# Unread products on TensorE ahead of both adjacency loops, the second transpositions and the self term

## The reference, cut to what matters

```python
def hgnn_layer(x, W, b, src, dst, w, c_in, c_out, n_nodes):
    h = hyp_linear(x, W, b, c_in)                  # product, then norms, tanh, artanh by node
    h = hyp_agg(h, src, dst, w, c_in, n_nodes)     # segment_sum(logmap0(h)[src] * w, dst)
    return hyp_act(h, c_in, c_out)

edge_index = jnp.stack([src, dst])
h = jnp.maximum(_layernorm(x, axis=-1), 0.0)
x = x + _L0_gnn_ref(h, edge_index, edge_weight, W0, b0, W1, b1)    # two layers
h = jnp.maximum(_layernorm(x, axis=-1), 0.0)
# messages: every edge and one self loop for each node, mean over the edges that arrive
edge_features = jnp.concatenate([x[src], x[dst]], axis=-1)
h = jax.nn.relu(edge_features @ W1 + b1)
edge_out = h @ W2 + b2
out = agg / jnp.clip(counts, 1.0)[:, None]
```

## Time and profile before

| | us |
|---|---|
| median of 3 runs | 1189.79 (1186.01, 1189.79, 1190.54) |
| the profiled execution | 1187.15 |
| its span, first to last instruction | 1185.4 |
| PE busy | 1030.4 (87%) |
| DVE busy | 1043.5 (88%) |
| ACT busy | 710.1 (60%) |
| POOL busy | 368.3 (31%) |

### The profile page before, as it was taken

One profiled execution on the slowest core, in us unless ns is written; L12 is line 12 of the kernel. 1 busy time (PEld: TensorE's weight loads), 2 busy tenths in 40 slices (PEclk: granted clock), 3 DMA queues, 4 the chain that ended last, 5 costly groups with the idle time before them and its releaser, 6 DMA issues.

```text
span 1185.4 us, 53710 instructions
## 1 busy us (share of the span) xinstructions
PE 1030.4 (87%) x21736; PEld 949.2 (80%) x21736; DVE 1043.5 (88%) x1435; ACT 710.1 (60%) x1934; POOL 368.3 (31%) x268
## 2 busy tenths in 40 slices
PE   3079898989898989828998599999999999999998
PEld 2057777777777777617998479999999999999997
DVE  8889999999999999285664889999999999999995
ACT  5348888888888888420002476665566555666663
POOL 7000000000000000100000037777777777777774
PEclk9589999999999999959998779999999999999999
DMA  2003222222223232669950255544444445444540
GB/s 82 0 33 126 96 118 103 110 111 104 116 97 124 95 126 95 265 250 337 408 243 23 81 171 164 161 158 153 156 158 157 159 159 161 161 161 161 161 161 29
DMA packets 44877, 169.98 MB, mean 143 GB/s; under 512 B 19440, under 2 KB 19766, under 8 KB 44827
## 3 DMA queue, kind: packets, MB, share of 16 engines
q1 hardware_dynamic: 44827, 169.28, 39.7%
HBM read 121.11 MB, written 48.14 MB: 143 GB/s over the span
## 4 chain that ended last, share of the span: by engine, by line
PE 53%; DVE 31%; issue 10%; DVEq 4%; ACT 2%; DMA 0%; POOL 0%; ACTq 0%; POOLq 0%
PE PS L1549 18%; PE PS L1551 12%; PE PS L1564 8%; PE PS L1424 8%; DVE arena L1050 6%; DVE arena L1027 6%; DVE arena L1035 4%; DVE arena L1013 3%; PE PS L1569 3%; DVE arena L1022 2%; DVEq L357 2%; PE PS L1502 1%; PE PS L1455 1%; PE PS L1531 1%; DVE aggTw L1061 1%
## 5 line engine op out<-in xcount | busy, mean ns | idle before, releaser
L590 POOL TENSOR_TENSOR arena<-arena 128x512 bf16<-128x512 f32 x240 | 341.9, 1441 | 324.2 <-ACT arena L768 324.2
L1549 PE MATMUL PS<-arena 125*128 125x128 bf16 x3600 | 343.9, 219 | 0.9
L768 ACT ACTIVATE arena<-arena 128x512 bf16<-128x512 f32 x240 | 150.8, 628 | 185.9 <-DVE arena L1272 185.9
L1549 PEld LDWEIGHTS PS<-arena 125*128 125x128 bf16 x3600 | 250.0, 97 | 7.3 <-issue 4.5
L1424 PE MATMUL PS<-arena,A 125*64 125x72 f32 x4800 | 180.0, 230 | 69.8 <-DVE aggTw L1061 40.7
L1424 PEld LDWEIGHTS PS<-arena,A 125*64 125x64 f32 x4800 | 166.1, 139 | 79.3 <-issue 53.6
L648 ACT ACTIVATE arena<-arena 128x72 bf16<-128x72 bf16 x864 | 217.0, 344 | 1.9 <-DVE arena L1035 1.9
L1272 DVE SCALAR_TENSOR_TENSOR arena<-PS,arena 128x512 f32<-128x512 f32 x240 | 159.6, 680 | 28.6 <-ACT arena L775 28.6
L775 ACT ACTIVATE arena<-PS 128x512 bf16<-128x512 f32 (+2 forms) x336 | 171.7, 546 | 1.4 <-PE PS L1551 1.4
L1551 PE MATMUL PS<-arena 108*128 108x128 bf16 x1200 | 167.0, 220 | 0.0
L1551 PE MATMUL PS<-arena,HTw 108*128 108x128 bf16 x1200 | 165.8, 219 | 0.0
(11 more groups left out here) (192 smaller groups left out, 1380.0 us busy)
## 6 DMA issues: line engine op xcount, KB each, us to landing
adjacency<-arena SPq DMA_DIRECT2D x48, 900.0 KB, 3.6
arena<-adjacency SPq DMA_DIRECT2D x46, 900.0 KB, 7.3
Bw<-slot_rows SPq DMA_DIRECT2D x48, 800.0 KB, 4.2
Cw<-slot_rows SPq DMA_DIRECT2D x48, 700.0 KB, 4.4
arena<-q_table SPq DMA_DIRECT2D x144, 18.0 KB
q_table<-arena SPq DMA_DIRECT2D x6, 336.0 KB
slot_rows<-slot_row SPq DMA_DIRECT2D x49, 13.0 KB
x_sb<-in_x SPq DMA_DIRECT2D x1, 700.0 KB
```

The lines of the kernel that those rows point to most:

```text
L590: nc.gpsimd.tensor_tensor(H3[k][:, at_b, 2, :], Hs[k][:, 4 * q:4 * q + 4, :], H3[k][:, at_b, 1, :], ALU.subtract).then_inc(s_low_set, 1)
L768: nc.scalar.activation(H3[k][:, at_b, 1, :], Hs[k][:, 4 * q:4 * q + 4, :], ACT.Copy).then_inc(s_mid_set, 1)
L1549: mm(ps, OTs[k][:, b, :], P3[:, b, part, :], start=(part == 0), stop=False)
```

## The change

A helper `keep_warm(n, at)` issues n products of 128x128 bf16 constants (`identb` and `onesb`) into columns 256 to 383 of one bank of PSUM. Nothing reads them. It is called at four places of PE's list:

- 50 ahead of the first adjacency loop, when DVE has passed the first step of the artanh series in `linear(0)` (semaphore `warm_linear`, 1);
- 50 ahead of the second adjacency loop, at the same place of `linear(1)` (`warm_linear`, 2);
- 50 ahead of `transposes(1)`, when DVE has done the first sums of the second layer norm (`warm_norm`);
- 12 ahead of the self term's first quad and 4 ahead of each of its six others, with no wait of their own.

```diff
+WARM = 50
...
-            def layer_norm(dst, source):
+            def layer_norm(dst, source, early=False):
 
                 for b in PIECES:
                     link(ve.tensor_reduce(row(T1)[:, b], source[:, b, :], X, ALU.add))
+                if early:
+                    ve.sem_inc(warm_norm, 1)
...
                 ts(row(ATN), row(T3), ARTANH[0], ALU.mult)
+                ve.sem_inc(warm_linear, 1)
                 for c in ARTANH[1:]:
...
-            layer_norm(A[:, :, :], x_sb[:, :, :])
+            layer_norm(A[:, :, :], x_sb[:, :, :], True)
...
+            def keep_warm(n, at):
+
+                for _ in range(n):
+                    mm(bank(at)[:, 256:384], identb[:, :], onesb[:, :], start=True, stop=True)
...
             pe.wait_ge(primed, 1)
+            pe.wait_ge(warm_linear, 1)
+            keep_warm(WARM, 6)
...
                 else:
+                    pe.wait_ge(warm_linear, 2)
+                    keep_warm(WARM, 6)
                     with pe.If(fast == 1):
                         second_groups(pe, second_body)
...
             last.then_inc(counts_ps, 1)
+            pe.wait_ge(warm_norm, 1)
+            keep_warm(WARM, 0)
             transposes(1)
...
             for c, bs in enumerate(QUADS):
+                keep_warm(4 if c else 12, 7)
                 pe.wait_ge(p_rest, c + 1)
```

More of the change, by code:

```diff
@@ L294, in gnn_kernel @@
         row_stored, p3_set = sem("row_stored"), sem("p3_set")
+        warm_linear, warm_norm = sem("warm_linear"), sem("warm_norm")
         any_idx, any_gathered, any_gathered_q = ([sem(f"{n}{i}") for i in range(3)] for n in (
```

## The result

The changed kernel takes 1196.08 us in the median of 14 runs (1185.81 to 1200.54), the kernel before 1187.66 in 14 on the same chip (1185.32 to 1190.54). The ratio is 1.006, with a 95% interval of 1.0043 to 1.0076: slower, and outside the range that I gave. The profiled execution took 1192.46, of which 1190.7 is the span, at a mean granted clock of 0.956; before it was 1187.15, 1185.4 and 0.953.

A forecast was written before the change was run, and what follows sets the result against it. PE led the chain with 53%, DVE had 31% and set the message loop's pace. Gains of 0.3 + 0.3 + 0 + 0 + 0 = 0.6 us from a mean of 1188.4 gave 1187.8 us, range 1183.5 to 1192.

The forecast's parts named there:

- Layer 1: Fifty fillers ahead of the first adjacency loop: 0.3 us gain taken, 1.8 if the clock stays up, -1.2 below.
- Layer 2: Fifty fillers ahead of the second adjacency loop: 1.1 us gain if the clock holds, -1.5 as opposite; 0.3 taken.
- Longer list: PE's list, 186 products longer, may add or remove a fetch stall in layer 2's first pass: -4.1 to +4.1 us, 0 taken.
- Transpositions: Second transpositions: Q begins up to 2.2 us earlier, worth 0 because DVE reads Q only at 673.53.
- Self term: Self term with fillers: 6.6 us instead of 10.4 if the clock holds, worth 0; 0.3 above, -1.0 if it stays low.
- fillers without effect: Rival: clock low at each start as before, self term with 2.7 us more PE work; 1189.4 us, chance 0.18.
- All four waits pay: Rival: the clock holds at all four places and PE's time counts in full, 8.9 us; 1179.5 us, chance 0.08.
- The longer list with two stalls: Rival: late instruction fetches stall PE in layer 2's first pass; one stall 1191.9 us, two 1196; chance 0.12.
- My mark for being wrong: DVE's wait for the DMA before the message loop gets shorter, or PE's new stalls in layer 2 exceed 4 us.

The follow-up runs named there:

- e8: Changed kernel without the fifty fillers ahead of each adjacency loop; those at the transpositions and self term stay: 1189.5 us, ratio 1.0011 to the kernel before.
- e1: Changed kernel without the 12 and 4 fillers in the self term; the three groups of fifty stay: 1190.68 us, ratio 1.0013 to the kernel before.
- e5: Changed kernel plus 20 fillers ahead of P's first quad and 4 ahead of each further one: 1190.8 us, ratio 1.003 to the kernel before.
- e7: Changed kernel with DVE reading Q ahead of the first group's one-hots and 45 instead of 12 fillers before the self term: 1187.44 us, ratio 0.9989.
- e10: Changed kernel with 100 fillers ahead of the first adjacency loop and none ahead of the second: 1194.52 us, ratio 1.0053 to the kernel before.
- e12: The changed kernel again, unchanged, as a control on the chip of e9 to e11: 1193.65 us, ratio 1.0055 to the kernel before.
- e9: Changed kernel with 64 instead of 50 fillers ahead of each adjacency loop: 1189.18 us, ratio 1.0012 to the kernel before.
- e4: Kernel before plus only the fifty fillers ahead of each adjacency loop: 1188.32 us, ratio 1.0.
- e2: Changed kernel without the fifty fillers ahead of the second transpositions: 1187.55 us, ratio 0.9996 to the kernel before.
- e3: Kernel before plus only the self term's 36 fillers: 1189.15 us, ratio 1.0004.
- e11: e7 with 64 instead of 50 fillers ahead of each adjacency loop: 1186.26 us, ratio 0.9986 to the kernel before.

## Why the prediction was wrong

The chain of causes, each link with what shows it:

1. The fifty at the transpositions raise the clock, these take 2.86 us, and Q is over earlier (after, e8).
2. The 100 fillers of the loops and these 50 move a fetch of instructions onto the start of the slot rows' load, which lands at 5.2 to 5.5 us instead of 4.3 to 4.5 (after, e1, e5, e7, e10, e12 against all the others; e9 moved it off the load and e10 kept it there, as expected). DVE's first read of Q comes three one-hots behind the landing.
3. PE stands 1.3 to 1.6 us between Q and P, and the clock falls by 2.3 us into P at the latest (after, e1, e10, e12; at 0.51 us it held, e8; with the gap filled or closed it held in spite of the late load, e5, e7).
4. The fillers in the self term then run on the low clock. They don't bring it up and make the stretch longer: 16.5 us for fillers and self term.
5. PE begins to spread 6.04 us late. Beyond the 1.15 us that it had to spare, this goes over ACT's relu copy to DVE's first split, which comes 4.9 us late. Nothing behind gives it back, as the loop has DVE's pace.

By the steps of the prediction:

- *Layer 1*, 0.3 of a possible 1.8: measured 0.16. The idleness of five microseconds cost the clock, as argued; the 1.8 was real, and e10 got it with 1.34 us of idleness (3.88 - 2.07).
- *Layer 2*, gain of 1.1 if the clock holds: it held and was 1.11. I had taken 0.3 as a mean over both cases, and the nine profiles bear that out: six held, three fell, 0.4 in the mean. e4 doesn't show it in the median.
- *Longer list*, 0 with 4.1 on each side: I had a late fetch, at the wrong place. I looked for stalls of PE in layer 2, where they went from 3.8 to 3.4 us, or from 4.3 to 3.4 with the counts' products (line 1455). The fetch cost where it met a load that DVE waits for, and between the transpositions and the loop PE has no wait for which the profile shows nothing. The Trainium skill ("Runtime: NRT & Kernel Launch", Instruction fetch mechanics) calls the cost of crossing a block of 16 KiB "mostly hidden". At this place the trace agrees for PE; for the load beside it the runs measured 0.7 to 1.2 us.
- *Transpositions*, 0 on the path: right that Q's earlier end brings nothing. The step failed in stopping there. An engine that is early at a gate it doesn't control is idle for as long, and on this chip idleness was then paid in P. I had even written that DVE reads Q "only at 673.53"; what PE does between Q's new end and that moment was the question to ask. For the transpositions' own clock the prediction had followed the trace and not the Trainium skill ("TensorE: Matmul & The Clock Gate", Part 4: PE-mode transpose), and that was right: 25 take 2.85 to 2.86 us when the clock is high at their start (I had said 2.4).
- *Self term*, worth 0, -1.0 at worst: **this is the step that failed.** Its path was right: PE late, ACT's relu copy late, the rest handed on to DVE's split. Its sizes were not. I had PE 2.7 us late and 1.0 handed on; measured are 6.04 and 4.89. The 24 fillers cost 4.7 us and not 2.7: from the first product to the first spreading product it is 15.06 us now and was 10.35. The 12 cost 1.4, where I had them covered by 1.04 us of idleness. That idleness was gone, since the bound took P as fast: P came 2.4 us earlier and took 9.23 instead of 5.77. And PE had 1.15 us to spare, not 1.7. At the high clock the price was too low as well, 6.6 us against 8.28 in e2. A wait of DVE for all seven quads of the self term stands in the program text (`self_ps`) and is now the long one, 8.78 us; I hadn't named it, but DVE's later wait for ACT shows that it did not decide.
- *The rivals*: fillers without effect, 1189.4, is what e1 to e4, e8 and e9 came to in their sum (1187.5 to 1190.7), with other mechanisms in it. All four waits pay was not seen in any run. The longer list with two stalls, 1196, meets the median of after by luck: the stalls that it counted did not grow.
- My mark for being wrong was a shorter wait of DVE for the DMA before the message loop. It is gone altogether, and PE's lateness stands in its place.

What stays open: why the executions of after lie so far apart (1185.81 to 1200.54, with mean clocks of 0.964 for the fastest and 0.949 for the slowest). Only one execution of each kernel has a trace. Over kernels with the same PE list up to there, layer 2 takes 135.0 to 143.8 us from its first product to the transpositions (e12, e5), and in it PE's waits for which the profile shows nothing sum to 2.3 and 7.2 us. So a good part of the scatter comes from there, whatever the fillers behind it do. Open is also why the clock fell in P after 1.3 to 1.6 us of idleness and not elsewhere after as much. The scatter of every kernel, 4 us and more, is larger than the gain that I had forecast.

## What to carry to other kernels

An engine that is made faster ahead of a gate which another engine holds gains nothing there and stands idle for as long; where its clock depends on being busy, ask what runs next on the low clock and who waits for that. For each such engine, list every wait in the program text of the stage, not only the ones that ended last in the trace, with the slack of each: here it was 1.15 us at DVE's first split. Here a few fillers between real products held a clock that was high and did not raise a low one; on the low clock they cost most. They also lengthen the list, which moves the fetches of instructions: where one meets a load on the path, a few instructions more or less can decide (28 products here, e12 against e9), so a change of this kind is tried at two lengths of the list.

## What was not expected of the hardware

- One packet of instructions (0.02 MB) at the start of a 700 KB load went with a landing at 5.2 to 5.5 us instead of 4.3 to 4.5 and a tail of single packets (six profiles against eight).
- With four products of 128 columns before each quad the high clock stayed up once it was there (e2, e3, e8); without any it fell inside the self term in e4. The same four on a low clock did not raise it in 16.5 us (after, e10, e12), while the loop's spreading products, 125 in a row, did after 3.1 to 4.0 us.
- An idle stretch of 1.3 to 1.6 us before P was followed by the fall in four profiles out of four, one of 0.51 us (e8) and none at all (e2, e3, e9) by no fall in P. The length alone doesn't decide: at layer 2's first group, with a second wait of 0.94 us inside it, the clock held after 1.56 to 1.67 us (after, e2, e4, e12) and was down by that second wait after 1.28 to 1.53 (e1, e5, e7). At the transpositions it held after 1.12 to 2.41 (after, e1, e5, e7, e8, e10, e11, e12) and fell after 2.10 (e9).
